# Second edge stage of a two-layer graph network kernel: another order of the steps on TensorE, ScalarE and VectorE

## The chip, the cores and the metric

The kernel runs on one core of a Trainium2 chip. The metric is the device time of one execution in microseconds (us), lower is better. The core has TensorE (PE, with its weight loads as PEld), VectorE (DVE), ScalarE (ACT), GpSimd (POOL) and SyncE (SP), each with its own instruction stream. They meet through semaphores alone.

## The reference, cut to what matters

100,000 nodes with 64 features, 50,000 edges sorted by destination. Two layers, each a residual and a layer norm around a graph layer:

```
messages = features[src] * edge_weight[:, None]
aggregated = segment_sum(messages, dst, num_segments=N_NODES)
out = act(features * aggregated @ W1 + b1) + act(aggregated @ W2 + b2)      # act: leaky ReLU
L0  = out * rsqrt(max(sum(out * out), L2_EPS))
x   = layernorm(x + L0)
...
messages = _ffn(x[dst], W1p, b1p, W2p, b2p) * edge_weights[:, None]         # two gelu layers
agg = segment_sum(messages, src, num_segments=num_nodes)
out = _ffn(concatenate([x, agg]), W1u, b1u, W2u, b2u)
x   = layernorm(x + out * rsqrt(max(sum(out * out), EPS_L2)))
```

## The kernel before, in words

Three stages follow each other. `first_edges` builds the aggregates of layer 0 in a table in HBM. `second_edges`, the stage that is changed, goes once over all nodes and all edges. `last_rows` computes the update of layer 1.

`second_edges` works in 98 windows. A window i has 12 groups of 128 rows in one tile `box[i % 6]`: 8 groups are plain node rows, loaded by SP, and 4 groups are the table rows of 512 edge ends, fetched by four indirect gathers that GpSimd issues. For all 12 groups the stage computes the new x of layer 0: `multiply` (features times aggregate, on VectorE, in place in `box`), `turn` (transposes on TensorE, into `turned_p`), `evict` (ScalarE, into `turned_s`), `products` (TensorE, into `z_p`), `slope` and `leak` (the two halves of the leaky ReLU, on ScalarE and VectorE, into `leaky`), `outputs` (TensorE, into `o_p`: sum of both branches, centred), `square`, `sum_outputs`, `roots`, `scale`, `add_rows`, `square_centred`, `sum_centred`, `roots` again, `normalize`. Turn, products, slope and leak come in three parts q = 0, 1, 2 of four groups each. SP stores the 8 plain groups. The 4 edge groups go on through the small network: `turn_neighbours`, `neighbours_in`, `first_product`, `first_gelu`, `second_product`, `second_gelu`, `join` (sums over equal nodes with a matrix from `first_edges`), `take` (ScalarE, into `ms`), and then four indirect scatters with addition, issued by GpSimd.

The order is written out by hand. Each of PE, ACT and DVE has a loop over rounds t, and `of(t, lag, what, ...)` issues the step `what` for window t - lag. Engines are strict about that order: a step that waits holds all that stand behind it. GpSimd's loop is: the four scatters of window k, then the four gathers of window k + 6. A scatter waits for `take` of its window, a gather for `add_rows` of the window that had the same `box`. The only step before the change that waits for the gathers is `multiply`, the last of its DVE round:

```
for k in range(NWIN):
    for h in range(HALVES):
        scatter(k, h)
        if k + SB < NWIN:
            gather(k + SB, h)
```

Which DVE steps read two operands from SBUF matters below. `multiply` (L729) reads `box` twice, `add_rows` (L776) reads `y` and `box`, `normalize` (L780) reads `y` and `root`. `leak` (L735) and `scale` (L770) read one operand from PSUM and one from SBUF.

## Time and profile before

| | us |
|---|---|
| median of three runs | 3018.17 (3011.1 to 3018.83) |
| the profiled execution: its own time | 3019.24 |
| its span, first to last instruction | 3017.4 |
| busy in the span: PE, DVE, ACT, POOL | 2161.6, 2204.7, 1066.6, 2383.8 |
| second edge stage: first gather to last scatter | 1279.03 to 2608.97 |
| indirect gathers and scatters of that stage | 392 and 392 |

Busy shares are means over three stages with different limits, so the stage must be read by itself. A row of the timeline gives start, duration, engine, line, operation, tiles, and in brackets the idle time of the engine before it and what ended that. "issue" means that the engine waited for nothing that the profile shows.

### The profile page before, as it was taken

The page shows a single profiled execution, that of the slowest core. Times are in us where ns is not written, and L with a number is a line of the kernel's source. Part 1 is how long each engine was busy: PE and PEld are TensorE (multiplying, and loading weights), DVE is VectorE, ACT ScalarE, POOL GpSimd, SP SyncE. Part 2 cuts the span into 40 slices and gives each one's busy share as a digit, 9 for nine tenths or more (in the row PEclk, how much of TensorE's full clock was granted, in tenths as well). Part 3 has the DMA queues.
Part 4 walks back from the last instruction along what each step waited for, and adds up shares of the span by engine and source line. Part 5 has one row for each costly group of instructions (what it writes and reads, how often), then busy time and mean ns, then how long its engine had stood idle before and what let it go on. Part 6 is the DMA issues. An engine that isn't in the chain of part 4 may idle for free. (4 is left out here: it accounts for less than half of the span.)

```text
span 3017.4 us, 39223 instructions
## 1 busy us (share of the span) xinstructions
PE 2161.6 (72%) x11956; PEld 1702.2 (56%) x11956; DVE 2204.7 (73%) x5529; ACT 1066.6 (35%) x1964; POOL 2383.8 (79%) x1774
## 2 busy tenths in 40 slices
PE   3046555555554553279898989989989998699997
PEld 3035555455454553257676666667667766466664
DVE  5079988888888886368777777777777777288888
ACT  0000000000000000045444444445445454288887
POOL 7678888888888888658888888888888887488888
PEclk8555555555555555589999999999999999699998
DMA  9898888888887766467776777776777676356664
GB/s 229 203 208 191 171 174 180 180 182 175 170 183 166 157 147 138 71 179 180 172 176 162 170 175 167 164 175 164 172 171 175 159 175 136 83 192 207 208 206 157
DMA packets 1036086, 516.47 MB, mean 171 GB/s; under 512 B 540544, under 2 KB 998336, under 8 KB 1035880
## 3 DMA queue, kind: packets, MB, share of 16 engines
q1 hardware_dynamic: 764616, 372.57, 47.1%
q0 software_dynamic: 144256, 77.17, 18.4%
q10 hardware_dynamic: 127008, 64.23, 7.5%
q8 instruction: 99, 1.62, 0.2%
q14 instruction: 107, 0.88, 0.1%
HBM read 269.97 MB, written 243.84 MB: 170 GB/s over the span
## 5 line engine op out<-in xcount | busy, mean ns | idle before, releaser
L300 PE MATMUL sums<-xg,weigh 128*128 128x64 f32 x1960 | 435.0, 418 | 518.0 <-ACT ms L323 380.9
L544 POOL DMA_INDIRECT state<-ms,sidx x392 | 657.2, 1677 | 157.4 <-issue 114.3
L256 POOL DMA_INDIRECT table<-ms,sidx x392 | 622.5, 1588 | 140.9 <-issue 115.2
L300 PEld LDWEIGHTS sums<-xg,weigh 128*128 128x128 f32 x1960 | 420.5, 327 | 551.7 <-issue 485.1
L368 DVE TENSOR_SCALAR weigh<-rowp,key,ew 128x128 f32<-128x128 f32 (+3 forms) x784 | 424.0, 603 | 167.7 <-PE rowp L288 160.1
L530 POOL DMA_INDIRECT box<-table,node_dst x392 | 397.7, 1015 | 128.6 <-issue 112.8
L243 POOL DMA_INDIRECT xg<-in_x,node_src x392 | 383.1, 977 | 120.8 <-issue 104.6
L323 ACT ACTIVATE ms<-sums 128x256 f32<-128x256 f32 x98 | 37.6, 384 | 1143.1 <-DMA table<-ms,sidx 1057.6
L374 DVE SCALAR_TENSOR_TENSOR seen<-rowp,key,earlier 128x128 f32<-128x128 f32 (+3 forms) x784 | 383.3, 544 | 0.0
L735 DVE SCALAR_TENSOR_TENSOR leaky<-z_p,bz,leaky 128x512 f32<-128x512 f32 x294 | 219.7, 748 | 212.4 <-ACT leaky L656 210.1
L577 PE MATMUL z_p<-turned_s,wz 128*128 128x512 f32 x588 | 325.9, 638 | 2.8 <-DVE leaky L735 1.6
L587 PE MATMUL o_p<-cenz,leaky 128*128 128x65 f32 x2352 | 286.0, 279 | 32.3 <-DVE leaky L735 32.0
L587 PEld LDWEIGHTS o_p<-cenz,leaky 128*128 128x128 f32 x2352 | 272.4, 193 | 47.6 <-DVE leaky L735 47.2
L568 PE MATMUL turned_p<-ident,box 128*128 128x128 f32 x1176 | 207.3, 306 | 126.8 <-DVE box L729 126.8
L288 PE MATMUL rowp<-ident,key 128*128 128x128 f32 x784 | 185.5, 417 | 128.4 <-DVE seen L374 121.5
L568 PEld LDWEIGHTS turned_p<-ident,box 128*128 128x128 f32 x1176 | 159.7, 160 | 197.6 <-issue 135.7
L623 PEld LDWEIGHTS ffo<-g,weigh_in 128*128 128x128 f32 x1960 | 239.7, 196 | 48.2 <-issue 45.3
L288 PEld LDWEIGHTS rowp<-ident,key 128*128 128x128 f32 x784 | 166.0, 240 | 129.1 <-DVE seen L374 122.3
L623 PE MATMUL ffo<-g,weigh_in 128*128 128x64 f32 x1960 | 235.9, 277 | 1.6 <-issue 1.6
L865 POOL TENSOR_TENSOR inv<-ssq,mhalf 128x8 f32<-128x8 f32 x98 | 160.9, 1642 | 73.6 <-DVE ssq L970 73.6
L656 ACT ACTIVATE leaky<-z_p,bz 128x512 f32<-128x512 f32 x294 | 193.6, 686 | 59.1 <-PE z_p L577 58.7
L729 DVE TENSOR_TENSOR box<-box 128x768 f32<-128x768 f32 x98 | 93.7, 956 | 131.8 <-DMA box<-table,node_dst 131.6
(93 smaller groups left out, 3553.4 us busy)
## 6 DMA issues: line engine op xcount, KB each, us to landing
box<-table SPq DMA_DIRECT2D x97, 768.0 KB, 5.0
joins<-weigh ACTq DMA_DIRECT2D x98, 640.0 KB, 3.8
weigh_in<-joins SPq DMA_DIRECT2D x98, 640.0 KB, 6.8
table<-rows SPq DMA_DIRECT2D x97, 512.0 KB, 5.3
pair<-state SPq DMA_DIRECT2D x97, 512.0 KB, 3.9
xin<-in_x SPq DMA_DIRECT2D x97, 256.0 KB, 6.1
state<-y SPq DMA_DIRECT2D x97, 256.0 KB
out<-y SPq DMA_DIRECT2D x97, 256.0 KB, 2.2
```

Of the source, the lines that this page charges most:

```text
L243: pool.indirect_dma_start(out=xg[:, i, :], out_offset=None, in_=x[:, :], in_offset=bass.IndirectOffsetOnAxis(ap=node[0][:, i:i + 1], axis= ...
L256: pool.indirect_dma_start(out=table[:, :], out_offset=bass.IndirectOffsetOnAxis(ap=sidx[0][:, i:i + 1], axis=0), in_=ms[k % MR][:, b, :], ...
L288: last = pe.transpose(rowp[n][k % 2][:, b * P:(b + 1) * P], key[n][:, i:i + 1].to_broadcast([P, P]), ident[:, :])
L300: last = pe.matmul(sums[k % 2][:, a * D:(a + 1) * D], block_of(0, k, b)[:, a * P:(a + 1) * P], xg[:, k * WT + b, :], start=b == a, stop=b ...
L368: last = dve.tensor_scalar(block_of(n, k, b), rowp[n][k % 2][:, (b + 1 - m) * P:(b + 1) * P], key[n][:, i:i + 1], ew[:, i:i + 1], ALU.is_e ...
L374: last = dve.scalar_tensor_tensor(out=seen[b][:, 0:m * P], in0=rowp[n][k % 2][:, (b + 1 - m) * P:(b + 1) * P], scalar=key[n][:, i:i + 1], ...
L530: pool.indirect_dma_start(out=box[i % SB][:, b, :, :].rearrange("p a f -> p (a f)"), out_offset=None, in_=table_rows[:, :], in_offset=bass ...
L544: pool.indirect_dma_start(out=state[:, :], out_offset=bass.IndirectOffsetOnAxis(ap=sidx[1][:, at:at + 1], axis=0), in_=ms[k % SM][:, b, :] ...
L568: last = pe.transpose(turned_p[n % 2][:, g * P:(g + 1) * P], box[i % SB][:, 4 * q + g, 0:2, :].rearrange("p a f -> p (a f)"), ident[:, :])
L577: pe.matmul(z_p[n % 2][:, :], wz[:, :], turned_s[q][:, :], start=True, stop=True).then_inc(z_up, 1)
L587: last = pe.matmul(o_p[:, b, g * M8:(g + 1) * M8], leaky[i % 2][r // 4][:, r % 4 * P:(r % 4 + 1) * P], cenz[:, :], start=True, stop=True)
L623: last = pe.matmul(ffo[:, (WT + a) * D:(WT + a + 1) * D], weigh[i % SW][:, at * P:(at + 1) * P], g2[i % 2][:, b * D:(b + 1) * D], start=b ...
```

## The change

Only the order of issue changes in the stage. No operation is added or removed. On DVE the two waits that `multiply` held (gathers and plain loads have landed) become a step `arrive` of their own. It stands at the same lag 0, just ahead of part 0 of `leak`. `multiply` comes a round later, `scale`, `add_rows` and `normalize` also come one round later, and between the three steps that read two SBUF operands others are set. On PE part 1 of `products` moves across the round's border, part 0 of `turn` stays after `outputs`, and `turn_neighbours` comes ahead of `outputs`. ACT follows.

```diff
 # tensor
                         for t in range(ROUNDS):
+                            of(t, 2, products, 1)
                             of(t, 5, second_product)
                             of(t, 2, products, 2)
                             of(t, 5, join)
+                            of(t, 4, turn_neighbours)
                             of(t, 2, outputs, 0)
                             of(t, 2, outputs, 1)
                             of(t, 1, turn, 0)
-                            of(t, 4, turn_neighbours)
+                            of(t, 4, first_product)
                             of(t, 1, turn, 1)
-                            of(t, 4, first_product)
+                            of(t, 1, turn, 2)
                             of(t, 1, products, 0)
-                            of(t, 1, turn, 2)
-                            of(t, 1, products, 1)
...
 # scalar
                             of(t, 2, slope, 1)
+                            of(t, 5, second_gelu)
                             of(t, 2, slope, 2)
                             of(t, 5, take)
+                            of(t, 4, neighbours_in)
                             of(t, 3, square_centred)
                             of(t, 2, square)
-                            of(t, 4, neighbours_in)
                             of(t, 1, evict, 0)
                             of(t, 1, evict, 1)
                             of(t, 4, first_gelu)
+                            of(t, 1, evict, 2)
                             of(t, 1, slope, 0)
-                            of(t, 1, evict, 2)
-                            of(t, 4, second_gelu)
...
 # vector
-                        def multiply(i):
+                        def arrive(i):
 
                             s = i % SB
                             dve.wait_ge(gathered[s], 16 * WT * (i // SB + 1))
                             dve.wait_ge(loaded[s], 16 * (i // SB + 1))
+
+                        def multiply(i):
+
+                            s = i % SB
                             dve.tensor_tensor(box[s][:, :, 1, :], box[s][:, :, 1, :], box[s][:, :, 0, :], ALU.mult).then_inc(multiplied, 1)
...
                         for t in range(ROUNDS):
+                            of(t, 2, leak, 1)
+                            of(t, 4, normalize)
+                            of(t, 3, scale)
+                            of(t, 1, multiply)
+                            of(t, 2, leak, 2)
+                            of(t, 3, add_rows)
                             of(t, 3, sum_centred)
                             of(t, 2, sum_outputs)
                             if 2 <= t < NWIN + 3:
                                 roots(t)
+                            of(t, 0, arrive)
                             of(t, 1, leak, 0)
-                            of(t, 1, leak, 1)
-                            of(t, 2, scale)
-                            of(t, 1, leak, 2)
-                            of(t, 3, normalize)
-                            of(t, 2, add_rows)
-                            of(t, 0, multiply)
```

On DVE, in a middle round of the stage, from the last of the root steps to the first of the next, the kernel before has these rows (`leaky_0`, `_1`, `_2` are the three parts; the wait for the gathers is inside the L729 row):

```order
L735 SCALAR_TENSOR_TENSOR leaky_0<-z_p,bz,leaky_0 128x512
L735 SCALAR_TENSOR_TENSOR leaky_1<-z_p,bz,leaky_1 128x512
L770 TENSOR_TENSOR y<-o_p,root 128x768
L735 SCALAR_TENSOR_TENSOR leaky_2<-z_p,bz,leaky_2 128x512
L780 TENSOR_TENSOR y<-y,root 128x768
L776 TENSOR_TENSOR y<-y,box 128x768
L729 TENSOR_TENSOR box<-box 128x12x64
L740 TENSOR_REDUCE v_0<-sq_y 128x12
L744 TENSOR_REDUCE v_0<-sq_o 128x12
```

After the change the same place reads so (line numbers move by four; the wait for the gathers now stands ahead of the `leaky_0` row):

```order
L739 SCALAR_TENSOR_TENSOR leaky_0<-z_p,bz,leaky_0 128x512
L739 SCALAR_TENSOR_TENSOR leaky_1<-z_p,bz,leaky_1 128x512
L784 TENSOR_TENSOR y<-y,root 128x768
L774 TENSOR_TENSOR y<-o_p,root 128x768
L733 TENSOR_TENSOR box<-box 128x12x64
L739 SCALAR_TENSOR_TENSOR leaky_2<-z_p,bz,leaky_2 128x512
L780 TENSOR_TENSOR y<-y,box 128x768
L744 TENSOR_REDUCE v_0<-sq_y 128x12
L748 TENSOR_REDUCE v_0<-sq_o 128x12
```

The three steps with two SBUF operands stood back to back. Now `scale` stands between `normalize` and `multiply`, and `leaky_2` between `multiply` and `add_rows`.

On PE, one round before, from `join` to `join` (`ffo` and `ffn` are the small network's tiles):

```order
L623 MATMUL ffo<-g_1,weigh_in 128x64 x10
L587 MATMUL o_p<-cenz,leaky_0 128x65 x4
L587 MATMUL o_p<-cenz,leaky_1 128x65 x4
L587 MATMUL o_p<-cenz,leaky_2 128x65 x4
L568 MATMUL turned_p<-ident,box 128x128 x4
L596 MATMUL ffn<-ident,y 128x128 x2
L568 MATMUL turned_p<-ident,box 128x128 x4
L603 MATMUL ffn<-nt_s,wp 128x256
L577 MATMUL z_p<-turned_s,wz 128x512
L568 MATMUL turned_p<-ident,box 128x128 x4
L577 MATMUL z_p<-turned_s,wz 128x512
L608 MATMUL ffo<-bp,ones 128x256
```

And after the change, the same stretch:

```order
L623 MATMUL ffo<-g_1,weigh_in 128x64 x10
L596 MATMUL ffn<-ident,y 128x128 x2
L587 MATMUL o_p<-cenz,leaky_0 128x65 x4
L587 MATMUL o_p<-cenz,leaky_1 128x65 x4
L587 MATMUL o_p<-cenz,leaky_2 128x65 x4
L568 MATMUL turned_p<-ident,box 128x128 x4
L603 MATMUL ffn<-nt_s,wp 128x256
L568 MATMUL turned_p<-ident,box 128x128 x8
L577 MATMUL z_p<-turned_s,wz 128x512 x2
L608 MATMUL ffo<-bp,ones 128x256
```

`turn_neighbours` (L596) moved ahead of `outputs` (L587), and the last two parts of `turn` (L568) stand together. In both orders L610, the last `z_p` row and the next `join` follow.

## Rows read from the trace of the kernel before

**Rows 1.** Busy time by stretch, from window 11's multiply to window 97's: us, then each engine.

```profile
1419.10:2556.20 1137.10, 1025.84 (x6190) 784.28 (x6189) 820.75 (x1806) 564.37 (x1032) 927.09 (x690) 0.94 0.73 168
```

**Rows 2.** The same view for L729 alone, two stretches: DVE busy, clock, DMA.

```profile
1360.60:1407.00 46.40, 3.80 (x4) 1.00 0.79 188
1419.10:2556.20 1137.10, 82.31 (x86) 0.94 0.73 168
```

**Rows 3.** Waits from 1409 to 2543 us: total us, times, longest.

```profile
POOL state L544 <- issue: 101.8, 334, 0.3
...
DVE box L729 <- DMA box<-table,node_dst: 85.3, 64, 2.6
...
POOL state L544 <- ACT ms L689: 3.0, 10, 0.3
```

**Rows 4.** Timeline of GpSimd alone: one round's scatters, first gather, next round's first scatter.

```profile
1988.06 1.63 POOL L544 DMA_INDIRECT state<-ms,sidx  x1 [0.30 <-issue]
1989.99 1.58 POOL L544 DMA_INDIRECT state<-ms,sidx  x1 [0.30 <-issue]
1991.87 1.57 POOL L544 DMA_INDIRECT state<-ms,sidx  x1 [0.30 <-issue]
1993.74 1.55 POOL L544 DMA_INDIRECT state<-ms,sidx  x1 [0.30 <-issue]
1995.60 1.02 POOL L530 DMA_INDIRECT box<-table,node_dst  x1 [0.30 <-issue]
...
2000.73 1.62 POOL L544 DMA_INDIRECT state<-ms,sidx  x1 [0.30 <-issue]
```

**Rows 5.** Timeline, around a fourth gather and the second scatter after it.

```profile
2024.87 0.94 DVE L780 TENSOR_TENSOR y<-y,root 128x768 f32<-128x768 f32 x1
...
2025.34 1.30 POOL L530 DMA_INDIRECT box<-table,node_dst  x1 [0.30 <-issue]
...
2028.38 0.96 DVE L729 TENSOR_TENSOR box<-box 128x768 f32<-128x768 f32 x1 [1.70 <-DMA box<-table,node_dst]
2028.88 1.93 POOL L544 DMA_INDIRECT state<-ms,sidx  x1 [0.30 <-issue]
```

**Rows 6.** Timeline: the steps of one round that follow on each other.

```profile
2000.58 0.74 DVE L735 SCALAR_TENSOR_TENSOR leaky<-z_p,bz,leaky 128x512 f32<-128x512 f32 x1
...
2001.38 2.89 PE L587 MATMUL o_p<-cenz,leaky 128*128 128x65 f32 x24 [0.32 <-DVE leaky L735]
...
2004.31 0.82 ACT L662 ACTIVATE sq_o<-o_p 128x780 f32<-128x780 f32 x1 [0.37 <-PE o_p L587]
...
2005.16 0.97 DVE L744 TENSOR_REDUCE v<-sq_o 128x12 f32<-128x780 f32 x1 [0.24 <-ACT sq_o L662]
...
2008.55 0.75 DVE L735 SCALAR_TENSOR_TENSOR leaky<-z_p,bz,leaky 128x512 f32<-128x512 f32 x1
...
2011.33 0.95 DVE L770 TENSOR_TENSOR y<-o_p,root 128x768 f32<-128x768 f32 x1
2012.20 0.74 DVE L735 SCALAR_TENSOR_TENSOR leaky<-z_p,bz,leaky 128x512 f32<-128x512 f32 x1
...
2012.86 0.95 DVE L780 TENSOR_TENSOR y<-y,root 128x768 f32<-128x768 f32 x1
```

**Rows 7.** Timeline: first scatter, last gather, take of window 93, take of window 97.

```profile
1336.15 1.93 POOL L544 DMA_INDIRECT state<-ms,sidx  x1 [26.16 <-ACT ms L689]
...
2552.21 0.94 POOL L530 DMA_INDIRECT box<-table,node_dst  x1 [0.30 <-issue]
...
2554.41 0.39 ACT L689 ACTIVATE ms<-ffo 128x256 f32<-128x256 f32 x1 [1.49 <-PE ffo L623]
...
2599.80 0.39 ACT L689 ACTIVATE ms<-ffo 128x256 f32<-128x256 f32 x1 [4.63 <-PE ffo L623]
```

**Rows 8.** Timeline near the stage's start, TensorE at its lower clock.

```profile
1309.16 5.39 PE L587 MATMUL o_p<-cenz,leaky 128*128 128x65 f32 x24 [1.56 <-DVE leaky L735]
```

**Rows 9.** Timeline near the stage's start: the first two multiplies.

```profile
1289.07 0.96 DVE L729 TENSOR_TENSOR box<-box 128x768 f32<-128x768 f32 x1 [42.54 <-DMA box<-table,node_dst]
...
1298.20 0.95 DVE L729 TENSOR_TENSOR box<-box 128x768 f32<-128x768 f32 x1
```

## The prediction

> **What bounds the kernel now.** Only the second edge stage is touched, so I read that stage, first by stretches. Over 86 rounds, from the multiply of window 11 to that of window 97, GpSimd is busy for 927.09 us in 690 instructions [rows 1]. Each has 0.30 us of issue before it [rows 3, 4], and 690 x 0.304 = 209.8 us. Together that is 1136.9 of 1137.1 us: GpSimd never rests. PE (1025.84) and DVE (820.75) do. The view of one line gives the rounds: 1137.1 / 86 = **13.22 us** a round, but 46.4 / 4 = **11.60 us** in the four early rounds in which the stock of six gathered windows was not yet used up [rows 2]. So PE, ACT and DVE could go a round in 11.6 us and are held at 13.2 by GpSimd. The waits say how: DVE's multiply waited 64 times, 85.3 us in all, for gathers, while GpSimd's scatters waited for `take` 10 times for 3.0 us, which is no more than their issue time [rows 3]. GpSimd is late, not starved.
>
> Then I look at GpSimd's own round. A clean one is 1988.06 to 2000.73, **12.67 us**, with scatters of 1.63, 1.58, 1.57, 1.55 and a first gather of 1.02 [rows 4]. The mean over the whole busy stretch, from the first scatter to the end of the last gather, is (2552.21 + 0.94 - 1336.15) / 92 = **13.23 us** [rows 7]. What makes 0.56 us? A fourth gather takes 1.30 where 0.95 is usual; it starts at 2025.34, inside a normalize that runs from 2024.87 to 2025.81. The second scatter takes 1.93 instead of 1.58; it starts at 2028.88, inside a multiply that runs to 2029.34 [rows 5]. In both cases the extra 0.35 is what was left of the DVE step (0.47, 0.46) less about 0.1. I went through all GpSimd instructions of the stage in this way: only normalize, multiply and add_rows stretch one, only if the GpSimd instruction **starts** inside them, and never leak, scale or the reductions. These three read two operands from SBUF. And the meeting isn't chance: multiply starts when the fourth gather has landed, 1.74 us after that gather's end (2026.64 to 2028.38), and the second scatter starts 2.23 us after it, so a late multiply always sits on that scatter.
>
> On this the Trainium skill speaks against the change (SBUF — State Buffer, "Who interferes with whom"): it has a DVE instruction with two SBUF inputs contend with GpSimd's reads, but it infers that descriptor generation needs the write interface and is therefore not stalled by a tensor_tensor. The row of 1.93 disagrees, as GpSimd does nothing but issue indirect DMAs there. By the page's inference the steady term below would be nil and only the two losses at the ends would remain.
>
> **The change, part by part.** No instruction is added, removed or resized; GpSimd's and SP's streams are the same. What can change is (a) GpSimd's stretches, (b) the round that the other engines need, (c) filling and draining.
>
> (a) I lay out a round that waits at `arrive`, counting from the end of the fourth gather. GpSimd's starts are then 0.30, 2.23, 4.11, 5.98, 7.84 and three later [rows 4]. `arrive` ends at 1.74 and leak 0 starts. One leak takes the engine 0.66 until the next step starts (2012.20 to 2012.86), a long step 0.87 (2011.33 to 2012.20) [rows 6]. So leak 1 starts at 2.40, normalize 3.06 (runs 0.95, to 4.01), scale 3.93, multiply 4.80 (to 5.75), leak 2 5.67, add_rows 6.33 (to 7.28). The three two-input steps hold 3.06-4.01, 4.80-5.75, 6.33-7.28, and GpSimd starts at 2.23, 4.11, 5.98, 7.84: **none is hit**, though the first is missed by only 0.1 us and the second by 0.23. As long as the rounds wait at `arrive`, GpSimd's round is the clean one, 12.67.
>
> (b) Do they wait? The new loop runs: leak 1, normalize, scale, multiply, leak 2: 0.66 + 3 x 0.87 + 0.74 = 4.01; outputs start 0.06 after (2001.32 to 2001.38) and take 2.93 until the square (2004.31), 0.85 until sum_outputs (2005.16), 3.39 for that and the roots until leak 0 (2008.55), 0.66 until leak 1 [rows 6]. Sum 4.01 + 0.06 + 2.93 + 0.85 + 3.39 + 0.66 = **11.9 us**, 0.3 longer than before, since leak 2 now stands behind multiply. That leaves 0.77 us a round against 12.67. It is thin, but nothing else I follow is later: slopes are ready before their leaks, turn 0 has its multiply 3 us early, sum_centred has its square 1 us before outputs' square. The normalize of window t-4 ends 1.8 us before turn_neighbours wants it, and a wait of SP for `add_rows` comes a half round later with rounds to spare. The price if the cover is gone: every us that the loop is longer than GpSimd's round is a us on each of 92 rounds.
>
> GpSimd isn't starved either. `take` now comes about 4.5 us after the previous window's `arrive` (z part 2, join, take), instead of 1.5 before its multiply. Of GpSimd's lag behind `take`, one round before, some 6 us remain.
>
> What steady round do I take? Clean 12.67. For the first nine rounds, until 0.7 us a round has used up the stock and the waits begin, hits fall as before: 9 x 0.56 / 92 = 0.05. A fall of TensorE's clock throws a round out of place. The granted clock was 0.94 of full, so at 1.2 GHz for 12% of the stretch [rows 1]; it fell behind the gather waits of some 1.7 us that stop TensorE. The new gaps of TensorE are smaller (0.6 ahead of z part 2, 0.4 ahead of outputs), so I take a quarter of the rounds displaced with half of the old stretch and more: 0.08. Together **12.80**. Bounds: 12.67 from below, 13.23 from above (as many hits as now). I stay near the lower one, as the layout gives no hit.
>
> Steady term: 92 x (12.80 - 13.23) = **-39.6 us**.
>
> (c) Start: GpSimd's long run begins at take of window 0, 1336.15 [rows 7]. The path to it has leaks 1 and 2 a round later, so about 6 us more, but its first round loses the leaks that filled 1289.07 to 1298.20 [rows 9], about 3 us. I take **+3** (0 to 6). End: between take 93 (2554.41, as the last gather lands) and take 97 (2599.80) lie 45.4 us without GpSimd's bound [rows 7]; take 93 will come about 4.5 us after `arrive` instead of just at it, and the drain is as long. I take **+5.5** (3 to 8).
>
> Sum: -39.6 + 3 + 5.5 = **-31 us**. From the profiled execution's 3019.2 (span 3017.4) that gives 2988; the median of the runs is 1 us lower, so I say **2987 us**.
>
> **The rivals.** (1) *The lock holds all the time.* TensorE stays at 2.4 GHz, the steady round is 12.70: 92 x -0.53 + 8.5 = -40, **2978**. For it: no gap over 0.6 us. Against: the loop's 0.77 us of slack is less than one half-clock outputs costs.
>
> (2) *The hits only move*, or they come from something else than the layout holds, such as the first miss of 0.1 us turning into a hit. Excess 0.35 to 0.56 a round: steady 13.02 to 13.23, -19 to 0, with the ends **3007 to 3027**. Against it: a hit at the very end of a normalize costs only its rest, a tenth of a us, not 0.35. By the page's inference above it would be the upper end.
>
> (3) *Slower: the loop becomes the bound.* Its place is outputs, which stood beside other work on DVE and now has leak 2 late ahead of it. At 1.2 GHz outputs takes 5.39 [rows 8] instead of 2.89, and the loop 14.4. If that befell more than half of the rounds, the mean would pass 13.15, and with +8.5 for the ends the kernel is slower. At three rounds in four the mean is 13.8: 92 x 0.55 + 8.5 = +59; at 0.6 of them 13.4, +24, **3042**. Against it: a clock of 0.94 now, with longer gaps.
>
> **How the numbers follow.** Chances: the forecast 0.53 (own range 2978 to 3002), rival 1 0.18, rival 2 0.18, rival 3 0.11. What a measurement of this kernel can tell is about 0.3%, 9 us: faster is under 3009, slower over 3027. Faster: 0.53 + 0.18 + a third of rival 2 = 0.77. Same: the rest of rival 2 = 0.12. Slower: 0.11. The range goes from rival 1 with every round clean and the ends at nothing extra (2967) to the middle of rival 2, 3015.
>
> **What would show it.** Right: GpSimd still at work without rest between first scatter and last gather, that stretch some 1178 us for 92 rounds instead of 1217; most second scatters at 1.58, fourth gathers at 0.95; DVE's gather wait ahead of leak 0, under 1 us each; granted clock above 0.94. The first scatter some 3 us later, take 97 some 50 us after the last gather. Wrong: GpSimd idle before scatters with ScalarE's `ms` as releaser (the loop is the bound), or third scatters stretched to 1.7 and more (the miss of 0.1 us failed), or a clock under 0.9.

## The result and the profile after

The changed kernel takes **3059.78 us** (median of four, 3047.04 to 3071.21) where the kernel before takes 3018.5 us: ratio **1.0135**, 95% interval 1.0104 to 1.0165. The prediction was 2987 us, 1.0% faster; the kernel is 1.35% slower. The profiled execution is the fastest of the four (3047.04 us, span 3045.3), so its trace shows a little less of the loss than the median has.

First GpSimd's two groups of instructions from 1370 to 2540 us (count, busy us and mean ns, idle time ahead and what ended it), then all engines in the stretch from the first scatter to the last gather, then the rows of that scatter and that gather:

```profile
L544 POOL DMA_INDIRECT state<-ms,sidx x346 | 553.4, 1599 | 123.0 <-issue 101.8 <-ACT ms L689 21.2
L530 POOL DMA_INDIRECT box<-table,node_dst x348 | 388.2, 1115 | 106.1 <-issue 93.0 <-DMA state<-ms,sidx 13.1
```

```profile
1339.50:2581.50 1242.00, 1133.56 (x6651) 879.37 (x6652) 878.64 (x1934) 618.45 (x1107) 998.80 (x736) 0.92 0.73 166
```

```profile
1339.56 2.13 POOL L544 DMA_INDIRECT state<-ms,sidx  x1 [29.75 <-ACT ms L689]
...
2580.44 0.95 POOL L530 DMA_INDIRECT box<-table,node_dst  x1 [0.30 <-issue]
```

Against [rows 7] the first scatter is 3.4 us later (+3 was predicted). The stretch is 1241.8 us, or **13.50 us a round** over 92 rounds, where it was 13.23 and 12.80 was predicted. That is +24.8 us. Stage three starts 28.4 us later than before (2646.29 for 2617.91), so filling and draining cost 3.6 together. GpSimd's eight instructions last 10.86 us a round in the mean (before 10.78, in a clean round of [rows 4] 10.23), eight issues are 2.43, and 0.21 us is now idle time, for `take`: 12 waits, 21.2 us with the issues in them, against 10 and 3.0 in [rows 3]. The granted clock of the stretch is 0.92, before 0.95. A hit is a GpSimd instruction that starts inside a VectorE step with two SBUF operands, and is stretched. Scatters are now nearly clean (1599 ns in the mean, before 1680; in 79 windows 13 first scatters are hit and no other), but the gathers are hit (1115 ns, before 1015). The hits have moved, not gone. Waits from 1370 to 2540 us:

```profile
PE z_p L577 <- DVE leaky L739: 74.2, 48, 2.3
DVE leaky L739 <- DMA box<-table,node_dst: 67.5, 43, 2.2
...
POOL state L544 <- ACT ms L689: 21.2, 12, 1.8
```

Two and a half rounds tell why. Timeline, from a first gather on; SPq rows are the issues of SP's three transfers (768, 640 and 256 KB):

```profile
1455.38 1.02 POOL L530 DMA_INDIRECT box<-table,node_dst  x1 [0.30 <-issue]
...
1457.75 0.95 DVE L780 TENSOR_TENSOR y<-y,box 128x768 f32<-128x768 f32 x1
...
1458.33 1.19 POOL L530 DMA_INDIRECT box<-table,node_dst  x1 [0.30 <-issue]
1458.73 0.36 SPq L499 DMA_DIRECT2D box<-table  x1
...
1459.13 0.58 SPq L504 DMA_DIRECT2D weigh_in<-joins  x1
1459.76 2.12 SPq L509 DMA_DIRECT2D state<-y  x1
1459.82 0.95 POOL L530 DMA_INDIRECT box<-table,node_dst  x1 [0.31 <-issue]
...
1467.09 1.41 DVE L739 SCALAR_TENSOR_TENSOR leaky<-z_p,bz,leaky 128x512 f32<-128x512 f32 x2 [2.08 <-DMA box<-table,node_dst]
1467.99 1.10 PE L577 MATMUL z_p<-turned_s,wz 128*128 128x512 f32 x2 [2.17 <-DVE leaky L739]
1468.42 0.95 DVE L784 TENSOR_TENSOR y<-y,root 128x768 f32<-128x768 f32 x1
1468.62 1.64 POOL L530 DMA_INDIRECT box<-table,node_dst  x1 [0.30 <-issue]
1468.92 4.24 PE L623 MATMUL ffo<-g,weigh_in 128*128 128x64 f32 x20
...
1470.15 0.95 DVE L733 TENSOR_TENSOR box<-box 128x768 f32<-128x768 f32 x1
1470.57 1.39 POOL L530 DMA_INDIRECT box<-table,node_dst  x1 [0.30 <-issue]
...
1473.38 5.22 PE L587 MATMUL o_p<-cenz,leaky 128*128 128x65 f32 x24
...
1489.14 2.13 POOL L544 DMA_INDIRECT state<-ms,sidx  x1 [1.81 <-ACT ms L689]
```

`add_rows` (1457.75) releases SP, whose load starts at 1458.73, **2.04 us before the fourth gather ends** (1459.82 + 0.95 = 1460.77). The first leak, behind the wait for that gather, starts at 1467.09: **6.3 us** after the gather's end, where 1.74 was assumed; over windows 12 to 96 the least is 5.52, the median 5.77. The trace also has the semaphore updates of the DMA queues: by them the fourth gather itself has landed 5.54 us after its end in the median, before the change 1.72. With it the three two-operand steps come over 4 us late and sit on the next gathers (1.64 and 1.39 for 1.02 and 0.98). TensorE stands 2.17 us, falls to half clock in the next row (join 4.24 for 2.34, outputs 5.22 for 2.89), and `take` comes too late for GpSimd, which rests 1.81 us at 1489. Before, the same burst lay among the scatters (the first of that round starts at 2000.73 [rows 4]), 5 us ahead of the first gather. There it held up no gather, and the scatters had time: they had landed 2.1 us after the last one's end, and GpSimd's next scatter, which waits for that, comes 5 us later:

```profile
2003.08 0.36 SPq L499 DMA_DIRECT2D box<-table  x1
...
2008.53 1.02 POOL L530 DMA_INDIRECT box<-table,node_dst  x1 [0.30 <-issue]
...
2012.40 0.95 POOL L530 DMA_INDIRECT box<-table,node_dst  x1 [0.30 <-issue]
```

GpSimd's reserve (from the end of `take` to the start of the first scatter of its window, the time by which GpSimd is behind) is 0.28 to 3.33 us, median 2.07; it was 14.1, and 6 was predicted. TensorE was at half clock for 204.8 us in 17 stretches between 1330 and 2550 us, 13 of them of 13.65 us; before for 126.3 us in 31 stretches of 3.4 or 6.8 us.

### The profile page after: what moved, and what is told of

Read it like the earlier page. It is cut to its first block and busy times, and to the rows that moved or that the text cites. A ratio compares the mean times of both kernels' runs of the same rounds, so it can differ in the third digit from the quotient of the medians.

```text
span 3045.3 us, 39223 instructions
## 1 busy us (share of the span) xinstructions
PE 2196.1 (72%) x11956; PEld 1741.3 (57%) x11956; DVE 2202.3 (72%) x5529; ACT 1081.0 (35%) x1964; POOL 2388.7 (78%) x1774
## 5 line engine op out<-in xcount | busy, mean ns | idle before, releaser
L544 POOL DMA_INDIRECT state<-ms,sidx x392 | 627.2, 1600 | 180.2 <-issue 113.6
L530 POOL DMA_INDIRECT box<-table,node_dst x392 | 433.7, 1106 | 128.6 <-issue 105.4
L577 PE MATMUL z_p<-turned_s,wz 128*128 128x512 f32 x588 | 301.4, 622 | 80.8 <-DVE leaky L739 76.9
L587 PE MATMUL o_p<-cenz,leaky 128*128 128x65 f32 x2352 | 322.4, 301 | 30.1 <-DVE leaky L739 30.1
L587 PEld LDWEIGHTS o_p<-cenz,leaky 128*128 128x128 f32 x2352 | 311.5, 216 | 50.3 <-DVE leaky L739 50.3
L623 PEld LDWEIGHTS ffo<-g,weigh_in 128*128 128x128 f32 x1960 | 269.2, 216 | 51.5 <-issue 51.1
L656 ACT ACTIVATE leaky<-z_p,bz 128x512 f32<-128x512 f32 x294 | 202.0, 687 | 188.3 <-PE z_p L577 187.4
L623 PE MATMUL ffo<-g,weigh_in 128*128 128x64 f32 x1960 | 264.9, 298 | 1.6 <-issue 1.6
L568 PE MATMUL turned_p<-ident,box 128*128 128x128 f32 x1176 | 198.5, 300 | 51.8 <-DVE box L733 44.6
L748 DVE TENSOR_REDUCE v<-sq_o 128x12 f32<-128x780 f32 x98 | 94.6, 966 | 156.2 <-ACT sq_o L662 156.2
L568 PEld LDWEIGHTS turned_p<-ident,box 128*128 128x128 f32 x1176 | 155.2, 160 | 84.2 <-DVE box L733 44.7
```

Of the source, the lines that this page charges most:

```text
L530: pool.indirect_dma_start(out=box[i % SB][:, b, :, :].rearrange("p a f -> p (a f)"), out_offset=None, in_=table_rows[:, :], in_offset=bass ...
L544: pool.indirect_dma_start(out=state[:, :], out_offset=bass.IndirectOffsetOnAxis(ap=sidx[1][:, at:at + 1], axis=0), in_=ms[k % SM][:, b, :] ...
L568: last = pe.transpose(turned_p[n % 2][:, g * P:(g + 1) * P], box[i % SB][:, 4 * q + g, 0:2, :].rearrange("p a f -> p (a f)"), ident[:, :])
L577: pe.matmul(z_p[n % 2][:, :], wz[:, :], turned_s[q][:, :], start=True, stop=True).then_inc(z_up, 1)
L587: last = pe.matmul(o_p[:, b, g * M8:(g + 1) * M8], leaky[i % 2][r // 4][:, r % 4 * P:(r % 4 + 1) * P], cenz[:, :], start=True, stop=True)
L623: last = pe.matmul(ffo[:, (WT + a) * D:(WT + a + 1) * D], weigh[i % SW][:, at * P:(at + 1) * P], g2[i % 2][:, b * D:(b + 1) * D], start=b ...
```

## The experiments

Theory A: SP's transfers among the gathers make them land late, and all else follows. Its rivals: the layout or the hits are wrong in themselves; GpSimd starves for want of windows in stock; the clock decides. The hold is a wait that keeps SP's transfers back until the gathers have landed. Ratios are against the kernel before on the same chip.

|  | chip | median us | ratio (95%) | round | reserve, median | idle before scatters | half clock (stretches) | gather landed, median | GpSimd's instructions |
| --- | --- | --- | --- | --- | --- | --- | --- | --- | --- |
| before |  | 3018.5 | 1 | 13.23 | 14.1 | 1 | 126 (31) | 1.72 | 10.78 |
| changed, shown above |  | 3059.78 | 1.0135 | 13.50 | 2.07 | 19 | 205 (17) | 5.54 | 10.86 |
| e1 | 6 | 2983.94 | 0.9884 (0.9868-0.9901) | 12.72 | 6.62 | 0 | 72 (4) | 1.67 | 10.28 |
| e2 | 6 | 3026.55 | 1.0027 (1.0017-1.0037) | 13.28 | 15.2 | 2 | 164 (12) | 4.48 | 10.82 |
| e3 | 6 | 2992.03 | 0.9909 (0.9892-0.9925) | 12.98 | 10.2 | 0 | 143 (25) | 4.97 | 10.53 |
| e4 | 6 | 2967.13 | 0.9831 (0.9815-0.9848) | 12.68 | 13.7 | 3 | 106 (17) | 1.68 | 10.21 |
| e5 | 9 | 3085.36 | 1.0173 (1.0145-1.0202) | 13.71 | 1.70 | 28 | 266 (24) | 5.54 | 10.97 |
| e6 | 9 | 3066.65 | 1.0112 (1.0083-1.0140) | 13.53 | 10.7 | 32 | 229 (30) | 1.69 | 10.76 |
| e7 | 9 | 3033.64 | 1.0018 (0.9996-1.0039) | 13.08 | 3.5 | 0 | 48 (5) | 1.49 | 10.64 |
| e8 | 9 | 3043.73 | 1.0034 (1.0015-1.0054) | 13.22 | 16.5 | 1 | 55 (8) | 1.55 | 10.78 |
| e9 | 7 | 3044.36 | 1.0030 (1.0009-1.0051) | 13.35 | 3.32 | 12 | 130 (13) | 1.54 | 10.79 |
| e10 | 7 | 3026.26 | 0.9966 (0.9953-0.9978) | 13.07 | 3.53 | 0 | 44 (5) | 1.49 | 10.64 |
| e11 | 7 | 3087.69 | 1.0179 (1.0155-1.0203) | 13.63 | 2.07 | 29 | 215 (19) | 5.53 | 10.89 |
| e12 | 7 | 3035.15 | 0.9988 (0.9972-1.0004) | 13.23 | 13.8 | 2 | 92 (21) | 1.57 | 10.79 |
| e13 | 1 | 3089.86 | 1.0161 (1.0144-1.0178) | 13.71 | 1.77 | 31 | 276 (21) | 5.49 | 10.94 |
| e14 | 1 | 3025.30 | 0.9960 (0.9934-0.9986) | 12.99 | 5.91 | 5 | 79 (8) | 1.50 | 10.49 |
| e15 | 1 | 3090.42 | 1.0166 (1.0149-1.0183) | 13.69 | 0.28 | 68 | 454 (83) | 1.63 | 10.52 |
| e16 | 1 | 3035.30 | 0.9977 (0.9967-0.9986) | 13.16 | 5.08 | 0 | 218 (16) | 1.50 | 10.70 |
| e17 | 3 | 2972.79 | 0.9859 (0.9842-0.9875) | 12.73 | 7.92 | 0 | 51 (5) | 1.69 | 10.28 |
| e18 | 3 | 3084.65 | 1.0224 (1.0207-1.0241) | 13.78 | 1.14 | 49 | 232 (16) | 5.52 | 10.81 |

The columns from "round" on are us, worked out from each trace as above. Round: first scatter to last gather's end over 92, with seven boxes over 91. Half clock: stretches that begin from 1330 to 2550 us, each counted whole; in e1, e3, e4 and e17 the last of them runs on into the end of the stage, and 40, 49, 24 and 24 us of the sum lie past 2550. Landed: the fourth gather's last semaphore update after its end, windows 12 to 96. Instructions: GpSimd's eight of a round, 1370 to 2540 us. With 2.43 us of issue and the idle time over 92 they make up the round in every run, to 0.03 us. The traces from chips 1, 7 and 9 have only 21 to 25 thousand semaphore updates of DMA queues where the others have over 38 thousand, so landings there are least values.

**e1, e9, e14: SP's transfers held until the gathers of window i - 3 have landed.** In SP's `load`, behind its wait for `added`:

```diff
+                            if i >= 3:
+                                sp.wait_ge(gathered[(i - 3) % SB], 16 * WT * ((i - 3) // SB + 1))
```

> The changed kernel, with SP's three transfers of a round (box load, join matrix, store) held until the fourth gather of the round has landed. Theory A (SP's transfers, which add_rows releases, now start 0.5 us before the gathers and hold up their landing): the fourth gather lands 1.7 us after its end again instead of 5.5, GpSimd's reserve behind take grows from 3.3 to 6 or 7 us, the two-input steps miss GpSimd's starts, a steady round of 12.7 to 12.9 us and 2980 to 3000 us in all. Theory B (the loop of TensorE, ScalarE and VectorE with its clock falls is the bound, and the late landing only goes with it): no change, 3045 to 3070 us.

Measured: 1.2% faster than before. Timeline of e1, from the third gather of a window:

```profile
1999.69 0.95 POOL L532 DMA_INDIRECT box<-table,node_dst  x1 [0.30 <-DMA state<-ms,sidx]
2000.95 0.95 POOL L532 DMA_INDIRECT box<-table,node_dst  x1 [0.30 <-issue]
2002.20 1.63 POOL L546 DMA_INDIRECT state<-ms,sidx  x1 [0.30 <-issue]
2003.73 0.36 SPq L501 DMA_DIRECT2D box<-table  x1
2003.76 1.41 DVE L741 SCALAR_TENSOR_TENSOR leaky<-z_p,bz,leaky 128x512 f32<-128x512 f32 x2 [0.86 <-DMA box<-table,node_dst]
2004.13 1.59 POOL L546 DMA_INDIRECT state<-ms,sidx  x1 [0.30 <-issue]
...
2005.09 0.95 DVE L786 TENSOR_TENSOR y<-y,root 128x768 f32<-128x768 f32 x1
...
2006.02 1.56 POOL L546 DMA_INDIRECT state<-ms,sidx  x1 [0.30 <-issue]
2006.82 0.95 DVE L735 TENSOR_TENSOR box<-box 128x768 f32<-128x768 f32 x1
...
2007.88 1.57 POOL L546 DMA_INDIRECT state<-ms,sidx  x1 [0.30 <-issue]
2008.35 0.95 DVE L782 TENSOR_TENSOR y<-y,box 128x768 f32<-128x768 f32 x1
```

The fourth gather ends at 2001.90 and the leak starts 1.86 later (median 1.76). From there the predicted layout stands, 0.13 us late: normalize 3.19 after the gather (predicted 3.06), multiply 4.92 (4.80), add_rows 6.45 (6.33), between GpSimd's starts at 2.23, 4.12 and 5.98. No scatter is stretched here (the third starts 0.02 us before normalize ends and takes 1.56), and over the stage the eight instructions last 10.28 us a round, where 10.23 is clean. The first term of the prediction was right but for its premise.

> The kernel of e1_burst_after_gathers once more, as the partner of the next run on one chip, since e7 and e1 ran on different chips. Theory A: 0.985 to 0.992 of the kernel before on this chip too. If the gain of e1 belonged to its chip, the ratio is above 0.995.

Measured in e9, on another chip: 1.0030. The gain over the kernel before did not repeat there. It is not a return of the late landing: the gathers landed 1.54 us after their end, and between windows 12 and 95 the first leak never waited for them, but 35 times for `slope`. As the rounds are not tied to the gathers, the steps slide onto GpSimd's starts again: its instructions last 10.79 us a round, 0.51 more than in e1, and with 0.13 of idle time that is the whole difference of the rounds. e14 was made to part chip and order:

> The changed order with SP's three transfers held until the gathers of window i - 3 have landed. Theory A: 1.2 to 2.5 per cent faster than the changed kernel on the same chip, whatever the chip; against the kernel before 0.988 where TensorE's results come when its records end, 1.000 to 1.003 where they come later. Rival B: the same time as the changed kernel within 0.3 per cent.

**e5, e13: the changed kernel again.**

> The changed kernel once more, for a second trace of it, since its runs lie 24 us apart and the traced one was the fastest. If GpSimd's small reserve is what spreads them, a slower run shows more rounds with the reserve at its least (a scatter that starts 0.3 us after its take) and more idle time of GpSimd before first scatters than the 19 us of the first trace, and landing late by 5.5 us as before. If something else spreads them, GpSimd's idle time stays at 19 us and its busy rounds are longer.

> The changed kernel once more, on the same chip as the three runs that follow, so that late transfers and the order as changed are compared without a change of chip. Theory A (SP's transfers among the gathers make the gathers land about 5.5 us late, which holds the whole loop): 1.3 to 1.8 per cent slower than the kernel before, the first part of leak 5 us or more behind the fourth gather's end in the median round. Rival B (the chip alone decides, the order is worth nothing on some chips): within 0.3 per cent of the kernel before.

Measured: 1.0173 and 1.0161, so the loss holds on each chip tried. In e5, whose trace is of a slower execution than the first one, GpSimd's idle time and its instructions have both grown. Beside e13, e14 is 64.6 us faster (2.1%) on one chip. That shows theory A; what the hold gives against the kernel before differs from chip to chip (0.988, 1.003, 0.996), and e14's 0.996 is outside the 1.000 to 1.003 that I had given for its chip.

**e2: a seventh box, SP released by the same window as before.**

```diff
-                SB, SY, SW, SM = 6, 4, 3, 3
+                SB, SY, SW, SM = 7, 4, 3, 3
-                            wait(sp, added, i - SB + 1)
+                            wait(sp, added, i - 5)
```

> The changed kernel with seven box buffers for the gathers in place of six; SP's loads are released by the same event as with six. GpSimd gets a round more of reserve. Theory A: the transfers still collide in part, but no clock fall reaches GpSimd, so it never waits for take; only the hits of the two-input steps remain, a steady round of 13.1 to 13.3 us, 3015 to 3030 us. Theory B: the loop is the bound whatever the reserve, 3045 to 3070 us, and GpSimd then waits for take or for free boxes for over 20 us.

Measured: GpSimd's idle time is gone (1.9 us) and the hits stay (round 13.28). The landing is late as before (4.48 us). So most of the loss is that GpSimd starves, the rest hits that did not go.

**e3, e12: the kernel before, with its transfers moved.** In SP's `load`, e3 (puts them among the gathers), then e12 (a hold like e1's, at a place where they hardly moved):

```diff
+                            if SB <= i:
+                                sp.wait_ge(leaked, 3 * (i - 4) + 1)
```

```diff
+                            if i >= SB:
+                                sp.wait_ge(gathered[(i - 4) % SB], 16 * WT * ((i - 4) // SB + 1))
```

> The kernel before, with SP's three transfers held until part 0 of leak of the next round, so that they start when the gathers do. Theory A: the fourth gather lands over 3.5 us after its end instead of 1.7; the reserve behind take was 13 us, so GpSimd does not starve and the time stays within 0.5% of 3018 us. Theory B (landing is late because the order is late, not because of transfers): landing stays at 1.7 us and the time at 3018.

> The kernel before with the same hold on SP's transfers as in e1 (until the fourth gather of the round has landed), a control. There the transfers already started within 1 us of that landing, with 5 us to the next gathers. Theory A: nothing to cure, within 0.3% of before. If holding SP back helps by itself, whatever the order: 1% faster, as in e1.

Measured in e3: the start of multiply after the fourth gather's end goes from 1.74 to 4.90 us at least, 5.55 in the median, in the old order. The cause of the late landing is shown from both sides. The time was missed: 0.9% faster, outside what I had expected. The late multiply now misses the second scatter (12 hits in 79 windows, before 68) and no fourth gather is hit (before 35); third and fourth scatters are hit in its place, and in sum the instructions are 0.25 us a round shorter. The old order has reserve enough (10.2 us) to bear the late landing. So that alone is not a loss; it is one where the reserve is thin. e12 is the control: no change.

**e4: the kernel before without second operands.** `multiply`, `add_rows` and `normalize` become reductions of one operand into spare tiles; the products, the sum with the features and the scaling by the root are left out.

```diff
-                            dve.tensor_tensor(box[s][:, :, 1, :], box[s][:, :, 1, :], box[s][:, :, 0, :], ALU.mult).then_inc(multiplied, 1)
+                            dve.tensor_reduce(spare[0][:, :], box[s][:, :, 1, :], AX_X, ALU.add).then_inc(multiplied, 1)
```

> The kernel before, with multiply, add_rows and normalize each replaced by a sum over one SBUF operand of the same 768 elements a partition and about the same 0.95 us; it leaves out the product with the features, the residual and the normalization of this stage. Hit theory (a step with two SBUF operands holds up a GpSimd instruction that starts inside it): scatters of 1.56 and gathers of 0.95 throughout, a steady GpSimd round of 12.7 us, 2965 to 2975 us. If the stretches come from elsewhere (the descriptor ring, the transfers): the second scatter stays at 1.9 and the time at 3018 us.

Measured: 0.9831, and GpSimd's groups (1370 to 2540 us) are clean:

```profile
L545 POOL DMA_INDIRECT state<-ms,sidx x372 | 587.4, 1579 | 124.0 <-issue 110.8 <-DMA state<-ms,sidx 11.3 <-ACT ms L690 1.9
L531 POOL DMA_INDIRECT box<-table,node_dst x359 | 349.4, 973 | 109.4 <-issue 104.2 <-DMA state<-ms,sidx 5.2
```

In the kernel before the means are 1680 and 1015. The hits are worth 0.55 us a round. The reductions also write less than the steps that they replace, so by itself e4 does not tell reading from writing. The traces do: `scale` writes as much as `normalize`, with one operand from PSUM, and of the GpSimd instructions of all twenty traces (from window 12 on) 717 start inside a `scale`; neither these nor any other that starts outside the two-operand steps takes over 0.05 us more than is usual. The 2505 that start inside one are stretched by about what is left of the step less 0.1 us (in the median by 0.24 where 0.3 to 0.4 is left, by 0.51 where 0.6 to 0.7 is). By the Trainium skill (SBUF — State Buffer, "Who interferes with whom") a tensor_tensor should not stall descriptor generation, which is inferred there. The measurement shows that it does stall an indirect DMA instruction. Such an instruction also reads its indices from SBUF (`sidx`, `node_dst`), and whether that reading or the descriptors are held up is not shown.

**e6: the wait for the gathers back at `multiply`, the rest as changed.**

```diff
+                            of(t, 1, arrive)
                             of(t, 1, multiply)
...
-                            of(t, 0, arrive)
```

> The changed kernel with arrive moved from ahead of part 0 of leak to right ahead of multiply of the same window, three DVE steps later. That gives GpSimd 3 us more of reserve and leaves TensorE's next products free of the wait, but multiply starts with the landing again. Theory A: the reserve is 5 us or more and GpSimd hardly waits for take; normalize and multiply meet the first and second scatter or, with the landing late, the third; 3015 to 3035 us. Theory B (where the wait stands among the steps doesn't matter, the loop is the bound): 3045 to 3070 us.

Measured: 1.0112, slower than I expected. The reserve is back (10.7 us), yet GpSimd stands 32 us ahead of scatters, put to issue and to landing scatters, never to `take`. The record says what it waits for. `scatter` has a second wait, that the scatters of the window before have landed, and SP's transfers have moved once more, onto these:

```profile
2013.39 1.62 POOL L544 DMA_INDIRECT state<-ms,sidx  x1 [0.30 <-issue]
...
2017.29 0.36 SPq L499 DMA_DIRECT2D box<-table  x1
...
2018.32 2.62 SPq L509 DMA_DIRECT2D state<-y  x1
2019.36 1.57 POOL L544 DMA_INDIRECT state<-ms,sidx  x1 [0.30 <-issue]
...
2027.03 1.62 POOL L544 DMA_INDIRECT state<-ms,sidx  x1 [1.00 <-issue]
```

They start 4.4 us after a first scatter (median), and the scatters have landed 4.6 us or more after the last one's end, where it is 1.6 us as changed and 2.1 before. `take` had ended 8 us or more ahead of each of these waits, so of the two waits it is this one; where the trace has the last landing, the scatter starts 0.77 us after it. The gathers landed on time (1.69 us) and the instructions are as before (10.76). So the whole loss of e6 (33 us, with 32 of idle time) stands at this wait. That the transfers make the landing late follows from where they start; no run of its own shows it.

**e7, e10: `scale` ahead of `normalize`, with the hold of e1.**

```diff
-                            of(t, 4, normalize)
                             of(t, 3, scale)
+                            of(t, 4, normalize)
```

> The kernel of e1_burst_after_gathers with two neighbouring DVE steps exchanged: scale ahead of normalize. Nothing else moves. Hit theory: normalize then runs 3.93 to 4.88 us after the fourth gather's end, the third scatter starts at 4.11 and is stretched by about 0.65 to 2.2 us in every round; the fourth then starts inside add_rows and is stretched too; a round of 13.3 to 13.9 us and 3040 to 3090 us. If e1 is fast for the transfers alone, and not because the two-input steps miss GpSimd's starts, the exchange costs nothing: 2980 to 2990 us.

> The kernel of e7 (e1's with scale ahead of normalize) beside e9 on the same chip. Hit theory: 25 to 45 us slower than e9, by stretched gathers or scatters at whatever place the round settles, with GpSimd never idle. If e7 was slow only for TensorE's late results on its chip (0.3 to 0.5 us on the mean there, none in e1), it is within 5 us of e9 here.

Measured: 1.0018 and 0.9966, rounds of 13.08 and 13.07 and no idle time: nearly each normalize now costs a first gather 0.35 (hit in 75 and 67 of 79 windows). On chip 7 this is still 18 us faster than e9, where 25 to 45 us slower was expected. The instructions say why: 10.64 us a round, in e9 10.79. The exchange brings one sure hit a round, and on this chip the order without it had more of them, in other places.

**e8: seven boxes and the hold of e1.** Both diffs above together.

> The kernel of e1_burst_after_gathers with seven box buffers. Its reserve was 6.6 us and GpSimd never waited for take, so by theory A a further buffer gives nothing: within 0.2% of e1, 2980 to 2988 us. If clock falls still reached GpSimd in e1's slower runs, it is 5 us or more faster.

Measured: 1.0034, round 13.22, on another chip than e1, so it is no direct pair. The hold did its work: in most rounds SP's load starts 1.7 to 1.9 us after the fourth gather's end, and the gathers have landed after 1.55. With 16 us of reserve, 1 us of idle time and no wait for gathers the instructions still last 10.78 us a round, as in e9: hits and not want of windows in stock. The loop of the other engines took 13.0 us in the median, not 11.9.

**e11: one bias product more in `second_product`.**

```diff
+                            pe.matmul(ffo[:, 0:WT * D], ones[:, :], bp2[:, :], start=True, stop=True)
```

> The changed kernel with one more product of the bias row in each second_product (its result is overwritten), 0.6 us of TensorE work ahead of the products that wait for part 0 of leak. If TensorE's idle time there makes its clock fall, and the falls are what uses up GpSimd's small reserve: less than half of the 205 us at the lower clock, GpSimd idle before scatters under 8 us, 15 to 30 us faster than the changed kernel (ratio to before 1.004 to 1.01). If the falls are not from that gap: no fewer of them, and the ratio stays at 1.0135 or goes above.

Measured: 1.0179, 19 falls of the clock and 29 us of idle time; nothing gained.

**e16: part 2 of `leak` ahead of `multiply`, with the hold of e1.**

```diff
-                            of(t, 1, multiply)
                             of(t, 2, leak, 2)
+                            of(t, 1, multiply)
```

> As the late transfers, and on VectorE part 2 of leak stands ahead of multiply, not behind it: outputs may start 0.9 us sooner in each round. multiply then ends at the start of a gather and add_rows follows it at once. Theory C: on a chip where the TensorE loop sets the round 15 to 60 us faster than the late transfers alone; where GpSimd sets it, one more stretched gather of 0.35 us in a round, 0 to 30 us slower. Rival: the loop runs through multiply and turn and not through outputs, then nothing is gained on either.

Measured: 10 us slower than e14 and 218 us at half clock instead of 79. GpSimd never rested, and its instructions last 10.70 us a round for 10.49: a shorter loop gained nothing, the hits cost.

**e15, e17: less work for TensorE, then the pause refilled, with the hold of e1.** e15: `join` leaves out six of ten products, the sums over equal nodes. e17 is e15 with `turn_neighbours` issuing its transposes seven times.

```diff
-                                for b in range(a, until):
+                                for b in range(a, a + 1):
...
+                            for _ in range(7):
                                 for q in range(2):
```

> As the late transfers, and join issues 4 instead of 10 products of 64 columns in a round (it leaves out the sums over equal nodes, so the messages are not joined). By the rows this takes 12 of 20 matmul records at 0.118 us, 1.4 us, out of TensorE's round. Theory C (with late transfers the TensorE loop is what sets the round on a chip with late results, 13.0 to 13.35 us against GpSimd's 12.7): the round falls to 12.7 us there, 30 to 60 us faster than the late transfers alone. Where GpSimd already sets the round (12.72 us measured) nothing or under 6 us is gained. Rival D (the clock's falls set it): more falls, no gain on any chip.

> As the short join with late transfers, and turn_neighbours issues its two transposes seven times (same input, same place), 12 more records of about 0.11 us, 1.3 us in all, in the pause that TensorE had ahead of outputs (1.64 to 1.87 us in the traces of the short join, each round, with 83 falls of the clock and 454 us at half clock). It leaves out the sums over equal nodes as that one did. Theory D (it is the pause ahead of outputs that the clock answers to, not the amount of work): falls in under 30 rounds, the round back under 13.2 us, 1 to 2.5 per cent faster than the short join alone. Rival C (the short join was slow for another reason, such as part 2 of leak coming later): no change within 0.5 per cent, 80 falls as before.

Measured: with **less** work for TensorE e15 is 65 us slower than e14, on the same chip. Its TensorE rows:

```profile
2013.52 1.00 PE L625 MATMUL ffo<-g,weigh_in 128*128 128x64 f32 x8
2014.36 0.39 PE L598 MATMUL ffn<-ident,y 128*128 128x128 f32 x2
2016.38 5.28 PE L589 MATMUL o_p<-cenz,leaky 128*128 128x65 f32 x24 [1.63 <-DVE leaky L741]
```

The time saved has become a pause of 1.63 us ahead of outputs in each round (in e14 the pause there is 0.33), and the clock falls 83 times. GpSimd waits 77.0 us for `take`. With useless transposes in the pause (e17) the same place reads:

```profile
2011.07 1.00 PE L626 MATMUL ffo<-g,weigh_in 128*128 128x64 f32 x8
2011.91 1.70 PE L599 MATMUL ffn<-ident,y 128*128 128x128 f32 x14
2013.97 2.89 PE L589 MATMUL o_p<-cenz,leaky 128*128 128x65 f32 x24 [0.36 <-DVE leaky L742]
```

Five falls, a round of 12.73 and a ratio of 0.9859: theory D of the expectation. The two ran on different chips, and part of the step from 1.0166 to 0.9859 is that: on chip 3, as on 6, TensorE's results come as its records end (below). The 83 falls against 5 are not explained by it, since e14 had 8 on e15's chip.

**e18: the changed kernel with its pause filled.** As e11, three bias products instead of one.

```diff
+                            for _ in range(3):
+                                pe.matmul(ffo[:, 0:WT * D], ones[:, :], bp2[:, :], start=True, stop=True)
```

> The changed kernel, and second_product writes its bias product three times more before the real one (same values), about 0.43 us each, 1.3 us in all. It stands just ahead of the pause of 1.64 us in which part 1 or 2 of products waits for the first part of leak and thus for the late gathers; the clock's falls of 13.65 us follow that pause in the trace. Theory D: the falls go from 17 to 24 in the stage to under 8, GpSimd's extra idle of 20 to 31 us is gone, 0.5 to 1 per cent faster than the changed kernel; hits of DVE steps on gathers stay, so it ends 0.3 to 1 per cent above the kernel before. Rival E (the idle time comes from the late landing alone): no gain, or slower by up to 1 per cent because the loop is longer.

Measured: 1.0224, the slowest of all; theory D fails here, and rival E holds: by the ratios it is 0.9% slower than the changed kernel. TensorE hardly stands any more (below, two rows that follow each other without a wait). It is busy for 1144.43 of 1170 us, and still 16 falls come, seven of them with no idle time over 0.1 us in the 28 us ahead:

```profile
2014.03 1.56 PE L609 MATMUL ffo<-bp,ones 1*128 1x256 f32 x6
2015.43 0.59 PE L610 MATMUL ffo<-bp,ones 1*128 1x256 f32 x2
```

Filling a pause with work is thus no safe remedy. The filler of e17 has the form 128*128, those of e11 and e18 1*128; whether that is the difference wasn't tried.

## Why the prediction was wrong

- **The step that failed** is in (b): "a wait of SP for `add_rows` comes a half round later with rounds to spare". It asked whether SP's data would be late, and not what its transfers would meet when they start. They moved by half a round, from among the scatters, which had time to land, onto the gathers. On that rests (a)'s premise "`arrive` ends at 1.74": 5.77 was measured, e1 restores 1.76, e3 brings 5.55 into the old order.
- **(a), the layout and the hits**: right, once the landing is right and the rounds wait for it (e1, e4). As changed, the hits fell on gathers: 10.86 us of instructions a round for 10.23.
- **(a), the clock's share** (0.08 us a round): too small. The pause of TensorE is 2.17 us in the round shown, not the 0.6 that was predicted, and the falls became longer (13.65 us, before 3.4 or 6.8).
- **(b), the loop at 11.9 us**: right where TensorE's results are on time (11.88 in rounds that wait for nothing). The prediction called its slack "thin", and that was right too: elsewhere the loop took 13.0 (e8, e9).
- **(b), the reserve of 6 us**: 6.62 in e1; as changed 2.07, four and a half less; the landing is 3.9 late. A fall of the clock costs a round about 4 us (join +1.9, outputs +2.3). That is under 6 and over 2: this is how the fault came to cost more than hits.
- **(c)**: start +3.4 for +3; the end nearly nothing for +5.5, a mis-sized term.
- **Steady term**: -39.6 predicted, +24.8 measured: +7 from instructions (0.08 us a round) and +18 from idle time and issue (0.20). The median execution is 13 us slower than the traced one.
- **The rivals**: the slower one was priced at 3042 and upwards with the loop as its place. Time and the sign "GpSimd idle before scatters with `ms` as releaser" came; its place, leak 2 ahead of outputs, did not. The wait came at `arrive`. Its sum does not come out either: with 14.4 and 12.67 us alone the mean passes 13.15 when 0.28 of the rounds are displaced, not half, and three in four give 13.97, so the rival was held to be rarer than its own prices say.

The case is settled for the loss. In part open is why the same kernel with the hold gives 0.988 on one chip and 0.996 to 1.003 on two others. The hits are where most of the time goes (instructions of 10.28, 10.49 and 10.79 us a round in e1, e14 and e9). Why they come back is not shown. There TensorE's results reach ScalarE later than its records end (below), and that is where I would put it.

## What to carry to other kernels

When a step moves, follow what it releases, on the DMA queues too, up to the row where the transfer starts, and look at what is landing then, and who waits for it: the gathers in the changed kernel, by the rows the scatters in e6. A reserve is what a displaced round costs, or it is nothing: here 6 us held against falls of 4 us and 2 us did not. On TensorE, taking out work that stands ahead of a wait makes a pause, and the pause can cost more than the work.

## What the runs showed of the hardware

- The four indirect gathers of a window (512 rows) had landed 1.7 us after the end of GpSimd's last instruction (kernel before, e1), 5.5 us after it where 1664 KB of SP's transfers were issued from 2 us before that end on (changed kernel), and 5.0 us where from 1 us before (e3).
- GpSimd's indirect DMA instructions are stretched when they start inside a VectorE step with two SBUF operands, by the rest of the step less about 0.1 us ([rows 5]: 0.35); 0.55 us a round in the kernel before (e4). Of over 10,000 that start outside such steps, inside `leak`, `scale` and the reductions too, none is (twenty traces).
- In the changed kernel most falls of the granted clock to 1.2 GHz lasted 13.65 us, in the short join (e15) 3.4 or 6.8 us. The longest pause of TensorE in the 28 us ahead of one was 1.4 to 2.3 us in the former, and the pauses were 1.63 us in the latter. What sets how long a fall lasts is not shown. The Trainium skill (TensorE: Matmul & The Clock Gate, "What's actually happening") has the gate follow how busy TensorE has been. e15 and e17 agree; e18, busy for 98% with 16 falls, does not fit so simply.
- In runs with the hold on chips 1, 7 and 9 TensorE's semaphore updates came 0.3 to 0.45 us after its records' ends in the mean (e15: 0.05), up to 3 us and more, on chips 3 and 6 0.01 us. The granted clock does not show it. These traces lack many records of semaphores, and may lack some of the clock, so how much of the lag is real is not shown; but in e9 ScalarE's `evict`, where it waits, does start 1.5 us after the end of the transposes' record, 0.25 in the kernel before. The kernel before takes 3034 to 3040 us on the former chips and 3018 on the latter.
